# The first layer's accumulator of value products is copied out of PSUM by VectorE instead of ScalarE

## The chip, the cores and the metric

The kernel runs on one core of a Trainium2 chip. The time is that of the device in microseconds, from start to end of one execution. Its engines work side by side, each with its own queue in fixed order, and wait for one another by semaphores: TensorE (PE in the profile, its weight loads PEld), VectorE (DVE), ScalarE (ACT), GpSimd (POOL) and SyncE (SP), which issues DMAs. PSUM is the memory that TensorE writes its results to, here eight banks of 128 partitions x 512 numbers of 4 bytes.

## What is computed

Two transformer layers over x of 16 batches x 512 tokens x 128 features, each attention plus a feed-forward part beside it:

```python
xn = layernorm(x)
x = x + attn0(xn) + ffn0(xn)   # 16 heads of 8, low-rank q/k/v with RMS norm, causal
xn = layernorm(x)
x = x + attn1(xn) + ffn1(xn)   # 16 heads of 8, a bias by position; composed weights, gelu
# in attention, per head: softmax(q @ k.T * scale + mask or bias) @ v, heads joined, projected
```

## The kernel before

The batches run one after another, a batch's work being spread over several "bodies" of 64 slots. A body is four head groups u = 0 to 3, each with four blocks of keys kt = 0 to 3, each with four steps j; slot 16u + 4kt + j. Every engine walks through the same slots by its own code and issues what is due there, so the order on each engine is written out by hand. For 14 bodies only the first layer runs, three more carry both layers in alternating slots, and the rest is the second layer alone. A slot of the first layer has

- on TensorE: at j = 0 the value products of the group before (L639, into pv_acc, one PSUM bank, 128 x 512; eight matmuls per block of keys), then a tile of scores transposed (L655, into one of three banks) and a tile of scores for the maxima (L680 and L692, into one of four banks);
- on ScalarE: the exponential of a bank of scores (L961, into probs);
- on VectorE: the reduction of a bank to row maxima (L1193, L1198, L1199, L1202, into maxs);
- on GpSimd: the causal mask on the probabilities (L1315).

The rest hangs on named slots: layernorm (L862 on ScalarE at slot 12), the transposes of the accumulator's copy (L705 on TensorE, named OA at slot 17 and OB at slot 49), the division by the row sums that follows (L1067 and L1074 on VectorE), the square root of the RMS norm (L897 on ScalarE at slot 42, which needs a table load before and after), the scaling by it (L1123 on VectorE at slot 43), the sum with x and its stores by GpSimd (L1281, L1283, L1259).

The value products of two head groups (a pair) add up in pv_acc. When the fourth block of the second group is done, at slot 12 (for the pair that ended with the body before) and at slot 44, the bank is copied to accS in SBUF. Only then may TensorE start the next pair there, at slots 16 and 48 (it waits for acc_taken), and transpose accS. The copy waits for the last value product and for the older transposes that read accS. There are two copies per batch and layer: 32 in the first, 32 in the second. A reduction of VectorE at slot 12 or 44 itself doesn't exist; the nearest ones come at slots 11, 13 and 15.

Of the kernel before, what the change touches and what calls it, by code (L numbers as in the profile page):

```python
# [21 lines left out]
NT = T // P  # L22
G = 4
NG = H // G
# [4 lines left out]
VW, PAIR = 32, 2  # L29
# [73 lines left out]
def max_column(j, qt):  # L103
    return 2 * NT * (j % E) + NT * (j // E) + qt


def place(layer, kt, j):

    if layer == 1:
        return G * kt + j, 0, T  # L110
    width = T - P * kt
    row, column = {0: (j, 0), 1: (G + j, 0), 3: (G + j, T - P), 2: (2 * G + j % 2, 2 * P * (j // 2))}[kt]
    return row, column, width
# [181 lines left out]
def wait(eng, sem, value):  # L295

    if not isinstance(value, int) or value > 0:
        eng.wait_ge(sem, value)
# [12 lines left out]
def build(nc, a, out):  # L311
# [14 lines left out]
    with ExitStack() as ctx:  # L326
        def sb(name, shape, dt=F32):
            return ctx.enter_context(nc.sbuf_tensor(name, shape, dt))
# [7 lines left out]
        acc = ctx.enter_context(nc.psum_tensor("pv_acc", [P, T], F32))  # L336
# [17 lines left out]
        accS = sb("accS", [P, T])  # L354
# [477 lines left out]
        def _(act):  # L832
# [8 lines left out]
            def body(B):  # L841
                s, layer = S[B.layer], B.layer

                full, taken = s["work_full"], s["act_taken"]
# [94 lines left out]
                for u in range(NG):  # L939
                    for kt in range(NT):  # L940
                        for j in range(G):
                            eo, eu = (-1, NG - 1) if u == 0 else (0, u - 1)
                            if j == 0 and kt == NT - 1 and u % PAIR == 0 and B.has(eo):
                                act.wait_ge(s["pv_done"], B.count(NG * NT, NT * eu + NT, eo))
                                if layer == 1 and B.number == 0 and u == PAIR:
                                    act.wait_ge(S[0]["work_full"], Body(0, LAST).use("OA").full)
                                if B.has(-1):
                                    transposed = B.use("OA") if u else Body(layer, B.number - 1).use("OB")
                                    act.wait_ge(full, transposed.full)
                                fn(accS[:], acc[:], ACT.Copy).then_inc(s["acc_taken"], 1)  # L950
                            number, pack, tile = TILES[layer][4 * kt + j]
                            if B.has(0) and tile == pack[-1]:
                                if layer == 0 and number == 0:
                                    wait(act, s["pv_done"], B.count(NG * NT, NT * (u - 1)))
                                if layer == 1 and B.number == 0 and u == 0 and number in (0, PACK_ROWS):
                                    act.wait_ge(S[0]["pv_done"], NG * NT * NB - (NT if number == 0 else 0))
                                if layer == 1 and j == 0:
                                    wait(act, s["pv_done"], B.count(NG * NT, NT * (u - 1) + kt + 1))
                                act.wait_ge(s["st_ready"], B.count(NG * EXPS[layer], EXPS[layer] * u + number + 1))
                                row = place(layer, *tile)[0] + (PACK_ROWS * (u % 2) if layer == 0 else 0)  # L960
                                fn(probs[:, row, :], st[:, B.use(("st", u, number)).bank, :], ACT.Exp, scale=SCALE  # L961
                                   ).then_inc(s["exp_done"], 1)
                            other(16 * u + 4 * kt + j)
                            yield

            run(body(Body(0, FIRST)))
            act.wait_ge(setup_pool, 5)
            run(body(Body(0, FIRST + 1)))
            act.wait_ge(stage_free, 3)
            run_first_layer(act, body)  # L970
            run_both_layers(body)
            run_second_layer(act, body)
# [4 lines left out]
        def _(dve):  # L977
            v = nc.vector
# [65 lines left out]
            def body(B):  # L1044
                s, layer = S[B.layer], B.layer

                full, taken = s["work_full"], s["dve_taken"]
# [129 lines left out]
                for u in range(NG):  # L1177
                    for kt in range(NT):
                        so, su = (0, u + 2) if u < 2 else (1, u - 2)
                        for j in range(NT):  # L1180
                            m = NT * kt + j
                            number, pack, tile = TILES[layer][m]
                            if layer == 1 and B.number + so == 0 and su < 2 and m == 0:
                                dve.wait_ge(S[0]["msplit"], 2 * NG * NB - 2 + 2 * su)
                            if B.has(so) and m == 0:
                                wait(dve, s["msplit"], B.count(2 * NG, 2 * (su - 1), so))
                            if B.has(so) and layer == 0 and tile == pack[-1]:
                                dve.wait_ge(s["s1_ready"], B.packs(0, su, number + 1, so))
                                bank = s1[:, Body(0, B.number + so).use(("max", su, number)).bank, :]
                                jh, qt = BESIDE[0][m]  # L1190
                                column = max_column(jh, qt)
                                if qt == 1:
                                    v.reduce_max(maxs[:, su % 2, column - NT:column + 1:NT],  # L1193
                                                 bank.rearrange("p (b n) -> p b n", b=2), AX_X
                                                 ).then_inc(s["red_done"], 1)
                                elif qt == 0:
                                    wide = max_column(jh, 2)
                                    v.reduce_max(maxs[:, su % 2, wide:wide + 1], bank[:, 0:3 * P], AX_X)  # L1198
                                    v.reduce_max(maxs[:, su % 2, column:column + 1], bank[:, 3 * P:T], AX_X  # L1199
                                                 ).then_inc(s["red_done"], 1)  # L1200
                                else:
                                    v.reduce_max(maxs[:, su % 2, column:column + 1], bank, AX_X  # L1202
                                                 ).then_inc(s["red_done"], 1)
                            if B.has(so) and layer == 1:
                                reduce_tiles(Body(1, B.number + so), su, m)
                            other(16 * u + 4 * kt + j)
                            yield

            for slot, _ in enumerate(body(Body(0, FIRST))):
                if slot == OTHER_WORK[0]["NORM"][0]:  # L1210
                    set_up()
# [188 lines left out]
```

## Time and profile before

| | |
|---|---|
| median of 3 runs | 1710.07 us (1704.68 to 1724.67) |
| profiled execution, its own time | 1698.95 us |
| its span, first to last instruction | 1697.2 us |
| mean granted TensorE clock | 0.974 of full speed |
| first layer alone | from about 100 to 700 us of the span |

The profile is of one execution. A row of a timeline gives the start in us from the start of the span and the duration in us; where several instructions of a line stand together, the duration is that of the group. The rows of one engine overlap a little: an instruction's end and the start of the next are pipelined. The bracket says how long the engine was idle before the row and whose work ended the idle time.

### The profile page before, as it was taken

What the parts mean: (1) busy time and instruction counts of PE and PEld (TensorE: products, weight loads), DVE (VectorE), ACT (ScalarE), POOL (GpSimd) and SP (SyncE); (2) the same over time, 40 slices, a digit from 0 to 9 for tenths busy, and PEclk for the clock granted to TensorE, in tenths of its full rate; (3) what the DMA queues carried; (4) which work ended last, traced back from release to release, by engine and by line L of the source; (5) the groups of instructions that cost most, each with busy time, mean ns of one, the idle gap of its engine ahead of it and who ended that gap; (6) DMA issues with size and microseconds to landing.
All of it is one profiled execution on the core that took longest, in us unless ns stands there. A gap on an engine that the chain in (4) does not pass through costs nothing.

```text
span 1697.2 us, 33267 instructions
## 1 busy us (share of the span) xinstructions
PE 1499.7 (88%) x11850; PEld 624.7 (37%) x11850; DVE 1378.8 (81%) x2538; ACT 1290.5 (76%) x2550; POOL 935.7 (55%) x1176
## 2 busy tenths in 40 slices
PE   4778888888888888888899999999999999999995
PEld 2644444444444444433233323233333323332331
DVE  2378888888888888888888898888888888889880
ACT  2258878878878787766788788888888888888884
POOL 2135555555555555554655655566556656565565
PEclk9879999999999999999999999999999999999998
DMA  8332332232222223322321223123321233122300
GB/s 289 63 57 76 76 73 76 76 73 79 76 75 74 78 64 74 81 63 49 79 70 51 57 53 68 57 51 57 64 66 51 48 64 74 51 58 48 67 15 19
DMA packets 133125, 116.41 MB, mean 69 GB/s; under 512 B 16856, under 2 KB 125664, under 8 KB 132960
## 3 DMA queue, kind: packets, MB, share of 16 engines
q1 hardware_dynamic: 126272, 100.64, 25.3%
q0 software_dynamic: 4096, 8.40, 1.5%
q10 hardware_dynamic: 2592, 5.24, 0.9%
q8 instruction: 95, 1.56, 0.4%
q14 instruction: 70, 0.57, 0.1%
HBM read 79.63 MB, written 33.55 MB: 67 GB/s over the span
## 4 chain that ended last, share of the span: by engine, by line
PE 53%; ACT 16%; DVE 14%; POOL 8%; issue 5%; DMA 3%; SPq 1%; DVEq 0%; POOLq 0%; ACTq 0%
PE pv_acc L639 16%; PE scores_transposed L655 13%; ACT probs L961 7%; PE scores_transposed L793 4%; PE scores_transposed L765 4%; PE scores_for_max L676 4%; DVE maxs L1171 3%; POOL x_between_layers L1259 2%; PE scores_for_max L801 2%; PE scores_for_max L705 2%; DVE maxs L1174 2%; POOL probs L1315 1%; DVE maxs L1202 1%; ACT xn L862 1%; POOL parts L1242 1%
## 5 line engine op out<-in xcount | busy, mean ns | idle before, releaser
L961 ACT ACTIVATE probs<-scores_transposed 128x512 f32<-128x512 f32 x1664 | 909.0, 600 | 178.3 <-PE scores_transposed L655 170.5
L655 PE MATMUL scores_transposed<-stacks 62*128 62x512 bf16 (+3 forms) x2048 | 583.5, 346 | 50.5 <-ACT probs L961 34.8
L639 PE MATMUL pv_acc<-probs,vals 128*32 128x512 f32 (+3 forms) x4096 | 469.3, 530 | 49.3 <-POOL probs L1315 25.4
L1341 POOL TENSOR_TENSOR probs<-probs,near_bias 128x512 f32<-128x512 f32 x256 | 329.6, 1290 | 327.0 <-ACT probs L961 326.1
L1171 DVE TENSOR_REDUCE maxs<-scores_for_max 128x2 f32<-128x1024 f32 x325 | 390.7, 1221 | 77.0 <-PE scores_for_max L676 76.3
L655 PEld LDWEIGHTS scores_transposed<-stacks 62*128 62x128 bf16 x2048 | 155.5, 94 | 603.8 <-ACT probs L961 304.0
L676 PE MATMUL scores_for_max<-stacks 60*128 60x512 bf16 x1024 | 328.7, 384 | 11.4 <-DVE maxs L1171 9.1
L1174 DVE TENSOR_REDUCE maxs<-scores_for_max 128x1 f32<-128x512 f32 x374 | 245.9, 684 | 16.1 <-PE scores_for_max L676 12.0
L680 PE MATMUL scores_for_max<-stacks 60*128 60x512 bf16 (+3 forms) x1024 | 248.9, 312 | 10.9 <-DVE maxs L1199 6.1
L1202 DVE TENSOR_REDUCE maxs<-scores_for_max 128x1 f32<-128x512 f32 x256 | 175.4, 685 | 82.4 <-PE scores_for_max L692 80.0
L1315 POOL TENSOR_SCALAR_AFFINE_SELECT probs<-probs 128x512 f32<-128x512 f32 x256 | 159.6, 638 | 76.7 <-ACT probs L961 76.4
L692 PE MATMUL scores_for_max<-causal_halves,ident_halves 64*128 64x128 bf16 (+2 forms) x1280 | 187.1, 233 | 0.0
L1198 DVE TENSOR_REDUCE maxs<-scores_for_max 128x1 f32<-128x384 f32 x256 | 140.2, 548 | 34.1 <-PE scores_for_max L692 33.2
L639 PEld LDWEIGHTS pv_acc<-probs,vals 128*32 128x32 f32 x4096 | 82.4, 108 | 159.7 <-issue 104.6
L692 PEld LDWEIGHTS scores_for_max<-causal_halves,ident_halves 64*128 64x128 bf16 x1280 | 112.9, 98 | 36.0 <-issue 5.1
L1242 POOL TENSOR_TENSOR parts<-rest,parts 128x512 bf16<-128x512 f32 x64 | 75.6, 1182 | 65.3 <-ACT parts L937 64.9
L676 PEld LDWEIGHTS scores_for_max<-stacks 60*128 60x128 bf16 x1024 | 77.6, 93 | 34.8 <-DVE maxs L1171 21.3
L1193 DVE TENSOR_REDUCE maxs<-scores_for_max 128x2 f32<-128x512 f32 x128 | 87.5, 684 | 0.9 <-PE scores_for_max L692 0.8
L680 PEld LDWEIGHTS scores_for_max<-stacks 60*128 60x128 bf16 x1024 | 77.6, 95 | 16.7 <-DVE maxs L1199 9.4
L1270 POOL TENSOR_TENSOR rstd<-mv,minus_half 128x4 f32<-128x4 f32 x32 | 33.4, 1042 | 82.5 <-DVE mv L1090 82.5
L1259 POOL DMA_INDIRECT out_dram<-x_new,slots_now x64 | 64.7, 1010 | 21.0 <-issue 10.6
L1259 POOL DMA_INDIRECT x_between_layers<-x_new,slots_now x64 | 65.1, 1017 | 17.0 <-issue 12.6
(131 smaller groups left out, 1982.8 us busy)
## 6 DMA issues: line engine op xcount, KB each, us to landing
stacks<-parts_scratch SPq DMA_DIRECT2D x768, 64.0 KB
parts_scratch<-parts SPq DMA_DIRECT2D x64, 384.0 KB, 2.6
x_tile<-in_L_attn_x_dram SPq DMA_DIRECT2D x16, 256.0 KB, 2.8
probs<-in_fc_B_dram ACTq DMA_DIRECT2D x1, 4096.0 KB, 19.5
stage_a<-in_fc_A_T_dram SPq DMA_DIRECT2D x1, 4096.0 KB, 16.8
stacks<-mT SPq DMA_DIRECT2D x256, 4.0 KB
x_res<-in_L_attn_x_dram SPq DMA_DIRECT2D x16, 256.0 KB, 3.3
x_tile<-x_between_layers SPq DMA_DIRECT2D x16, 256.0 KB
```

Of the source, the lines that this page charges most:

```text
L639: last = mm(acc[VW * j:VW * j + VW, q0:T], columns[:, first:first + VW], probs[:, row, column:column + width], start=(kt == 0 and pu % PAI ...
L655: last = mm(st[:, bank, column:column + T - q0], ks[p][rows, h, P * kt:P * kt + P], qs[p][rows, h, q0:T], start=True, stop=True)
L676: mm(bank, qs[p][rows, h, P * qt:P * qt + P], ks[p][rows, h, :], start=True, stop=True).then_inc(s["s1_ready"], 1)
L680: mm(bank[:, column:column + P * (qt + 1)], qs[p][rows, h, P * qt:P * qt + P], ks[p][rows, h, 0:P * (qt + 1)], start=True, stop=False, ski ...
L692: last = mm(masked, ident_halves[half, n, :], mask, start=False, stop=(n == 1), skip_group_check=True)
L961: fn(probs[:, row, :], st[:, B.use(("st", u, number)).bank, :], ACT.Exp, scale=SCALE).then_inc(s["exp_done"], 1)
L1171: v.reduce_max(maxs[:, su % 2, :].rearrange("p (e x) -> p e x", e=E)[:, :, column], s1[:, bank - 1:bank + 1, :], AX_X).then_inc(s["red_don ...
L1174: v.reduce_max(maxs[:, su % 2, column:column + 1], s1[:, bank, :], AX_X).then_inc(s["red_done"], 1)
L1202: v.reduce_max(maxs[:, su % 2, column:column + 1], bank, AX_X).then_inc(s["red_done"], 1)
L1259: g.indirect_dma_start(x_dst[layer], bass.IndirectOffsetOnAxis(slots_now[:, layer, t:t + 1], 0), x_new[:, t, :], None).then_inc(s["x_store ...
L1315: g.affine_select(out=diag, in_=diag, compare_op=ALU.is_ge, fill=0.0, base=0, pattern=[[0, G], [1, P]], channel_multiplier=-1).then_inc(s[ ...
L1341: g.tensor_tensor(diag, diag, near_bias[:, kt, :].unsqueeze(1).broadcast_to([P, G, P]), ALU.mult).then_inc(s["emul_pool"], 1)
```

## The change

The 32 copies of the first layer go from ScalarE's loop to VectorE's, at the same slots (kt = 3, j = 0, even u), ahead of what either engine does in that slot, with the same waits. The second layer's stay on ScalarE.

```diff
--- before.py
+++ after.py
@@ -940,7 +940,7 @@
                     for kt in range(NT):
                         for j in range(G):
                             eo, eu = (-1, NG - 1) if u == 0 else (0, u - 1)
-                            if j == 0 and kt == NT - 1 and u % PAIR == 0 and B.has(eo):
+                            if layer == 1 and j == 0 and kt == NT - 1 and u % PAIR == 0 and B.has(eo):
                                 act.wait_ge(s["pv_done"], B.count(NG * NT, NT * eu + NT, eo))
                                 if layer == 1 and B.number == 0 and u == PAIR:
                                     act.wait_ge(S[0]["work_full"], Body(0, LAST).use("OA").full)
@@ -1178,6 +1178,13 @@
                     for kt in range(NT):
                         so, su = (0, u + 2) if u < 2 else (1, u - 2)
                         for j in range(NT):
+                            eo, eu = (-1, NG - 1) if u == 0 else (0, u - 1)
+                            if layer == 0 and j == 0 and kt == NT - 1 and u % PAIR == 0 and B.has(eo):
+                                dve.wait_ge(s["pv_done"], B.count(NG * NT, NT * eu + NT, eo))
+                                if B.has(-1):
+                                    transposed = B.use("OA") if u else Body(layer, B.number - 1).use("OB")
+                                    dve.wait_ge(full, transposed.full)
+                                v.tensor_copy(accS[:], acc[:]).then_inc(s["acc_taken"], 1)
                             m = NT * kt + j
                             number, pack, tile = TILES[layer][m]
                             if layer == 1 and B.number + so == 0 and su < 2 and m == 0:
```

VectorE around slot 44 of a first-layer body, before (maxs are the reductions, the L1123 row the scaling by the root, L1067 the reciprocal of the row sums):

```order
L1110 SCALAR_TENSOR_TENSOR ffn<-fc,scores_for_max 128x512
L1123 TENSOR_TENSOR big<-big,rrms 128x4x256
L1198 TENSOR_REDUCE maxs<-scores_for_max 128x1
L1199 TENSOR_REDUCE maxs<-scores_for_max 128x1
L1198 TENSOR_REDUCE maxs<-scores_for_max 128x1
L1199 TENSOR_REDUCE maxs<-scores_for_max 128x1
L1202 TENSOR_REDUCE maxs<-scores_for_max 128x1
L1067 RECIPROCAL rsum<-scores_for_max 128x32
```

The same place after (the reductions' lines are 7 higher):

```order
L1110 SCALAR_TENSOR_TENSOR ffn<-fc,scores_for_max 128x512
L1123 TENSOR_TENSOR big<-big,rrms 128x4x256
L1187 COPY accS<-pv_acc 128x512
L1205 TENSOR_REDUCE maxs<-scores_for_max 128x1
L1206 TENSOR_REDUCE maxs<-scores_for_max 128x1
L1205 TENSOR_REDUCE maxs<-scores_for_max 128x1
L1206 TENSOR_REDUCE maxs<-scores_for_max 128x1
L1209 TENSOR_REDUCE maxs<-scores_for_max 128x1
```

The copy now stands between the scaling and four reductions.

ScalarE around slot 12, before (xn is the layernorm's result, vals the values for the next batch):

```order
L878 ACTIVATE fd<-scores_transposed 128x512
L961 ACTIVATE probs<-scores_transposed 128x512 x2
L950 ACTIVATE accS<-pv_acc 128x512
L862 ACTIVATE xn<-x_tile,minus_mean_rstd,rstd 128x128 x4
L961 ACTIVATE probs<-scores_transposed 128x512 x2
```

The same place after:

```order
L878 ACTIVATE fd<-scores_transposed 128x512
L961 ACTIVATE probs<-scores_transposed 128x512 x2
L862 ACTIVATE xn<-x_tile,minus_mean_rstd,rstd 128x128 x4
L961 ACTIVATE probs<-scores_transposed 128x512 x2
L889 ACTIVATE vals<-big 128x64x8
```

The copy is gone from between the exponentials and the layernorm. TensorE's order is the same in both kernels.

## Rows read from the trace of the kernel before

**Rows 1.** The page, busy time per engine (us, share of span, instructions).

```profile
PE 1499.7 (88%) x11850; PEld 624.7 (37%) x11850; DVE 1378.8 (81%) x2538; ACT 1290.5 (76%) x2550; POOL 935.7 (55%) x1176
```

**Rows 2.** View by tile, accS: duration in ns min/median/max; who waited (us, times).

```profile
L950 ACT ACTIVATE accS<-pv_acc x64: 591/598/628, 134.5 to 1678.7; 128x512 f32<-128x512 f32 x64
...
  PE pv_acc L639: 23.0, 14
```

**Rows 3.** View by line, L1030: the same read by VectorE, in the setup.

```profile
L1030 DVE COPY w<-pv_acc x1: 685/685/685, 50.7 to 50.7; 128x512 f32<-128x512 f32 x1
```

**Rows 4.** Chain that ended last, slots 43 to 48, body 4 (start us, us, what).

```profile
306.34 0.50 ACT accS L950
306.84 0.14 issue
306.98 1.06 PE pv_acc L639 x8
```

**Rows 5.** VectorE's timeline, same stretch (start, us, engine, line, instruction, [idle before <-releaser]).

```profile
305.20 1.22 DVE L1123 TENSOR_TENSOR big<-big,rrms 128x1024 f32<-128x1024 f32 x1
306.33 0.55 DVE L1198 TENSOR_REDUCE maxs<-scores_for_max 128x1 f32<-128x384 f32 x1
...
308.56 0.69 DVE L1202 TENSOR_REDUCE maxs<-scores_for_max 128x1 f32<-128x512 f32 x1 [0.81 <-PE scores_for_max L692]
```

**Rows 6.** TensorE's timeline, same stretch.

```profile
306.98 1.06 PE L639 MATMUL pv_acc<-probs,vals 128*32 128x512 f32 x8 [1.87 <-ACT accS L950]
```

**Rows 7.** VectorE's timeline, the same slots of body 3.

```profile
264.28 0.55 DVE L1198 TENSOR_REDUCE maxs<-scores_for_max 128x1 f32<-128x384 f32 x1
```

**Rows 8.** TensorE's timeline, the same slots of body 3.

```profile
260.23 0.28 PE L680 MATMUL scores_for_max<-stacks 60*128 60x256 bf16 x1 [0.66 <-DVE maxs L1199]
...
264.38 1.06 PE L639 MATMUL pv_acc<-probs,vals 128*32 128x512 f32 x8 [1.33 <-ACT accS L950]
```

**Rows 9.** Chain that ended last, slots 11 to 17 of body 5.

```profile
327.07 0.49 ACT accS L950
327.56 1.51 ACT xn L862 x4
329.08 0.50 ACT probs L961
...
329.62 0.28 PE scores_transposed L655
```

**Rows 10.** VectorE's timeline, same stretch.

```profile
327.14 0.56 DVE L1198 TENSOR_REDUCE maxs<-scores_for_max 128x1 f32<-128x384 f32 x1
...
329.44 0.69 DVE L1202 TENSOR_REDUCE maxs<-scores_for_max 128x1 f32<-128x512 f32 x1 [0.88 <-PE scores_for_max L692]
330.53 0.36 DVE L1067 RECIPROCAL rsum<-scores_for_max 128x32 f32<-128x32 f32 x1 [0.39 <-PE scores_for_max L705]
```

**Rows 11.** TensorE's timeline, same stretch.

```profile
327.86 1.07 PE L639 MATMUL pv_acc<-probs,vals 128*32 128x512 f32 x8 [0.54 <-POOL probs L1315]
328.86 0.39 PE L655 MATMUL scores_transposed<-stacks 62*128 62x512 bf16 x1
...
329.62 0.28 PE L655 MATMUL scores_transposed<-stacks 62*128 62x256 bf16 x1 [0.28 <-ACT probs L961]
...
329.84 0.66 PE L705 MATMUL scores_for_max<-ident,accS 128*128 128x128 f32 x4
```

**Rows 12.** Busy us (instructions) of PE, PEld, DVE, ACT, POOL; PEclk; DMA share; GB/s.

```profile
348.60:354.60 6.00, 5.03 (x34) 2.21 (x35) 3.79 (x10) 3.33 (x7) 4.08 (x6) 0.72 0.01 3
```

**Rows 13.** TensorE's timeline, the wait at slot 48 of bodies 5 and 6.

```profile
349.57 1.64 PE L639 MATMUL pv_acc<-probs,vals 128*32 128x512 f32 x8 [1.86 <-ACT accS L950]
...
393.70 1.07 PE L639 MATMUL pv_acc<-probs,vals 128*32 128x512 f32 x8 [1.26 <-ACT accS L950]
```

**Rows 14.** VectorE's timeline where both layers run, around slot 12 of body 15.

```profile
765.67 0.55 DVE L1198 TENSOR_REDUCE maxs<-scores_for_max 128x1 f32<-128x384 f32 x1
```

**Rows 15.** TensorE's timeline, same stretch.

```profile
765.51 1.07 PE L639 MATMUL pv_acc<-probs,vals 128*32 128x512 f32 x8 [0.47 <-issue]
```

## The prediction, written before the changed kernel ran

> **What bounds the kernel now.** I read the busy time per engine first [rows 1]: TensorE 88%, VectorE 81%, ScalarE 76% of the span. No engine is full, so the place of the moved work decides, not its amount. The view by tile comes next [rows 2]: one copy on ScalarE takes 598 ns (median), and TensorE has waited for it 14 times, 23.0 us in all. VectorE has done the same instruction once, in the setup, in 685 ns [rows 3]. Then the chain that ended last. Followed stretch by stretch through the first layer, it has 23 of the 32 first-layer copies on it, each with about 0.50 us of its own [rows 4, 9]; the rest of a copy's 0.6 us overlaps its neighbours. Read alone this says: take 23 x 0.5 = 11.5 us off the chain. The timelines of VectorE and TensorE around the copies tell how much of it really comes back. There are two kinds of copy in each batch. I call the one at slot 12 early and the one at slot 44 late.
>
> **The late copy (slot 44).** ScalarE makes it right after the two table loads around the square root, and TensorE stands still until it is done: 1.87 us before the value products of slot 48 [rows 6]. These start 0.14 us after the copy's end [rows 4]. Now where would VectorE put it? Behind the scaling by the root (L1123) and ahead of the reductions of slot 45. VectorE had no idle time in front of that place: L1123 starts at 305.20 and the next reduction at 306.33 [rows 5]. So the copy would start at 306.33, end 0.685 later at 307.02, and with the same 0.14 the products start at 307.16 instead of 306.98: 0.18 us later. ScalarE's freed 0.5 us buys nothing here, since it waits for TensorE's next scores anyway. In eight of the fourteen late copies before the two layers overlap the distance is this one (the reduction comes 0.09 to 0.13 after the old copy's start; losses 0.18 to 0.22, together 1.6 us). In five, bodies 1, 3, 6, 12 and 13, VectorE is 0.56 us later than that relative to ScalarE, TensorE too (its wait is 1.26 to 1.33 instead of 1.85). Body 3: the reduction starts at 264.28, so the copy ends at 264.97 and the products start at 265.11 instead of 264.38 [rows 7, 8]: 0.73 lost. VectorE is the later one there, TensorE had waited for one of its reductions before [rows 8]. The five lie between 0.73 and 0.79, together 3.8 us. Body 0 lies between them with 0.36. Late copies together: **+5.7 us**. The five were not on the chain, so up to 0.3 of each loss may be slack: 4.2 is the lower bound. What follows doesn't hide it: the chain goes on from these products through the transposes and the parts of Q and K to the next batch. VectorE has room for the longer queue: it idles 0.81 us before the reduction at 308.56 [rows 5].
>
> **The early copy (slot 12).** ScalarE makes it between an exponential and the four layernorm instructions of L862, all on the chain [rows 9], and TensorE waits 0.28 us for the exponential behind them [rows 11]. VectorE would start the copy at 327.14, where it now starts a reduction [rows 10], and end at 327.83; 0.14 on, the value products of slot 16 start at 327.97 instead of 327.86, where they now wait for GpSimd's mask [rows 11]. That is 0.11 lost on TensorE. But the exponential ends 0.49 earlier, so the scores of slot 17 come at 328.86 + 0.11 + 0.23 (two such score matmuls in a row start 0.23 apart) = 329.20 instead of 329.62: 0.42 gained. The transposes of accS start as much earlier, 329.42 for 329.84, and end at 330.08. VectorE meanwhile has its reductions 0.60 later, its wait of 0.88 at 329.44 shrinks, and the reduction there (329.55, 0.60 to the next start) frees it at 330.15. Its reciprocal of the row sums starts then, instead of 330.53 [rows 10]: 0.38 gained. The chain goes on from there through GpSimd's sum and stores, which were waiting for VectorE. The pattern is the same to 0.01 us in all 13 early copies of bodies 1 to 13. Early copies: 13 x 0.38 = **-4.9 us**.
>
> **Where both layers run (five copies, bodies 14 to 16).** At body 15 the products of slot 16 start at 765.51 with no wait for the copy. VectorE reaches its place only at 765.67 [rows 14, 15], so they would start at 765.67 + 0.69 + 0.14 = 766.50, a loss of 0.99. The other four lose 0.1 to 0.3 or nothing by the same rule, and ScalarE's freed time is on the chain once more, at body 16 (about -0.3). I take **+1.1 us**. The bounds: -2.5 (five times 0.5 freed) to +3.
>
> **The waits that move with the copy.** VectorE now waits for the value products of slot 44 or 12 and for an older transpose. Both are long past: TensorE is already idle [rows 6], or past its slot 15 [rows 11]. Behind the waiting instruction on VectorE stand the reductions of slots 13 and 15, whose banks TensorE needs again only from slot 49 (17) on. ScalarE loses these waits and gains nothing, as they weren't binding. TensorE, GpSimd, the DMA queues and layer 1 keep their instructions.
>
> **Sum.** +5.7 - 4.9 + 1.1 = **+1.9 us**, on the profiled execution's 1698.95: 1700.9. The three runs shown are 1704.68, 1710.07 and 1724.67, all above the profiled one, so I carry the difference to their median: 1710.07 + 1.9 = **1712 us**. About 1% (17 us) is what a measurement of this kernel can tell from no change, and this is far inside.
>
> The page "VectorE: DVE Perf Modes" of the Trainium skill, in its section on the TRN2 errata, gives 120 + N cycles at 0.96 GHz for VectorE's read of PSUM and 172 + N at 1.2 GHz for ScalarE's, and says that ScalarE sits closer to PSUM. For 512 columns that is an estimate of 658 and 570 ns, so it speaks against this move by 88 ns a copy; this case's rows have 685 and 598, 87 apart. By the page's 658 the sum would be 1 us smaller; the rows decide.
>
> **Rivals.**
> (a) ScalarE's relief carries in full and VectorE's later copy is made good, because its queue before slot 44 moves up too: 11.5 us gained at most, and with the late copies merely free the early 4.9: 1698.5 to 1705. For it: the chain's own shares. Against it: VectorE had no idle time before 305.20, and that queue begins behind TensorE's work, which moves with everything else.
> (b) The early gain doesn't carry, since another chain of the same length (GpSimd's masks, the stores) is close behind: the early copies then cost 0.11 each, 1.4 us, and the sum is 5.7 + 1.4 + 1.1 = 8.2: 1718. For it: the wait of TensorE there is only 0.28. Against it: GpSimd waits for VectorE's result in that place.
> (c) TensorE's clock, the case that is slower. At the late copy it idles 1.3 to 1.87 us, and with the change 2.05 in all fourteen (1.87 + 0.18, 1.33 + 0.73). After three of the fourteen waits, all three among those of 1.82 to 1.87 us, the clock was at 1.2 GHz for some us: mean 0.72 of full speed in 6 us [rows 12], the eight-matmul group 1.64 instead of 1.06 [rows 6, 13]. It cost about 1.5 us: body 5 to 6 took 393.70 - 349.57 = 44.13 us [rows 13], body 3 to 4 306.98 - 264.38 = 42.60 [rows 6, 8]. If it fell at all fourteen, 11 more x 1.5 = 17 us come on top: 1729, slower by 1.1%. It decides from the point where the idle time or the thin stretch ahead of it is a little longer. Against it: five more waits of the same 1.85 us left the clock alone. The Trainium skill's page "TensorE: Matmul & The Clock Gate", Part 1, has the clock gated by how busy the engine has been of late, and idle gaps drop it to the lower level; the trace agrees as far as its three falls go, and the rule points to this rival.
> (d) The copies don't move. The order of the instructions excludes it: 32 copies less on ScalarE, 32 more on VectorE.
>
> **How the numbers follow.** Forecast, the sum within 4 us: 0.50. (a) 0.18, (b) 0.15, (c) 0.12 (half of it with only some falls, 1715 to 1722), none of them 0.05. The range runs from 1698, which takes in (a) nearly whole and the lower bound of the mixed stretch, to 1724, which takes in (b) and a third to a half of the extra falls of the clock. Faster by over 1% would need 17 us, more than all copies give: 0.04, for what I don't see. Slower by over 1%: 0.10, from (c) and from (b) with VectorE's delay passed on everywhere. Within 1%: 0.86.
>
> **What the profile after would show.** Right: copies of 0.68 us on VectorE; TensorE's wait before the late products at 2.05 us in nearly all batches, ended by VectorE's copy; no wait of TensorE for the exponential at slot 17; 42.4 us from batch to batch where the late copy cost 0.18, and 43.0 where it cost 0.75; ScalarE 19 us less busy, VectorE 22 us more. Wrong: TensorE's wait before the late products under 1.8 us (VectorE's queue moved up, a), reciprocals no earlier against the exponentials (b), a granted clock well below 0.974 (c). What could upset all of it: that which makes VectorE 0.56 us later in five batches may come in none or in all fourteen, which is worth -2.9 to +5 us.

## The result, and the profile after

| | before | after |
|---|---|---|
| median | 1710.11 us of 16 runs (1698.32 to 1728.06) | 1722.25 us of 16 runs (1715.44 to 1736.35) |
| ratio, 95% interval | 1 | 1.009 [1.0066, 1.0113] |
| profiled execution, its span | 1698.95, 1697.2 us | 1721.62, 1719.8 us |
| granted TensorE clock | 0.974 | 0.965 |

A ratio, here and below, is that of the executions within 1.5% of the fastest of their kernel, so it isn't always that of the medians beside it. The change costs 12 us, 0.9%. The forecast had 1712.0 within 1698 to 1724, and no difference that a measurement can tell. The page after, busy time per engine, answers to [rows 1]:

```profile
PE 1510.0 (88%) x11850; PEld 628.7 (37%) x11850; DVE 1400.5 (81%) x2570; ACT 1275.4 (74%) x2518; POOL 932.0 (54%) x1176
```

VectorE has 21.7 us more, ScalarE 15.1 less, and TensorE, whose instructions are the same, is 10.3 us busier. That is the first sign of where the time went: the same matmuls took longer. The view by tile, accS, answers to [rows 2]:

```profile
L1187 DVE COPY accS<-pv_acc x32: 679/680/683, 129.6 to 840.0; 128x512 f32<-128x512 f32 x32
...
  PE pv_acc L639: 28.6, 14
```

TensorE waits for the copy in the same 14 places, 28.6 us instead of 23.0. At the late copy of body 3, the chain after, which answers to [rows 4]:

```profile
261.02 0.61 DVE accS L1187
261.63 0.14 issue
261.77 1.06 PE pv_acc L639 x8
```

VectorE and TensorE there, answering to [rows 5, 6]:

```profile
259.81 1.22 DVE L1123 TENSOR_TENSOR big<-big,rrms 128x1024 f32<-128x1024 f32 x1
260.94 0.68 DVE L1187 COPY accS<-pv_acc 128x512 f32<-128x512 f32 x1
261.54 0.54 DVE L1205 TENSOR_REDUCE maxs<-scores_for_max 128x1 f32<-128x384 f32 x1
```

```profile
261.77 1.06 PE L639 MATMUL pv_acc<-probs,vals 128*32 128x512 f32 x8 [2.05 <-DVE accS L1187]
```

The copy begins behind the scaling without idle time, 0.83 later come the products, and TensorE has waited 2.05 us, all as forecast. It is 2.05 or 2.06 in 13 of the 14 batches. The early copy, VectorE and TensorE at slots 12 to 17 of the next body, answering to [rows 10, 11]:

```profile
281.89 0.68 DVE L1187 COPY accS<-pv_acc 128x512 f32<-128x512 f32 x1
...
284.89 0.36 DVE L1067 RECIPROCAL rsum<-scores_for_max 128x32 f32<-128x32 f32 x1
```

```profile
282.68 1.06 PE L639 MATMUL pv_acc<-probs,vals 128*32 128x512 f32 x8 [0.57 <-POOL probs L1322]
...
283.91 0.28 PE L655 MATMUL scores_transposed<-stacks 62*128 62x256 bf16 x1
...
284.19 0.66 PE L705 MATMUL scores_for_max<-ident,accS 128*128 128x128 f32 x4
```

TensorE's wait for the exponential at slot 17 is gone (the row at 283.91 has no bracket), and the reciprocal starts 0.70 after the transposes' start, where it was 0.69 [rows 10, 11].

Then the stretches behind the late copies, 10 us each from 1.8 us ahead of the products (busy us and instructions of PE, PEld, DVE, ACT, POOL; PEclk; DMA share; GB/s), as in [rows 12], bodies 3 to 5:

```profile
259.97:269.97 10.00, 8.20 (x90) 4.22 (x91) 9.01 (x20) 7.80 (x16) 5.82 (x8) 1.00 0.08 27
302.24:312.24 10.00, 8.20 (x67) 3.74 (x68) 7.66 (x16) 6.49 (x13) 5.43 (x8) 0.83 0.01 2
346.03:356.03 10.00, 8.20 (x50) 3.68 (x51) 6.79 (x14) 5.82 (x12) 5.38 (x8) 0.66 0.01 2
```

The clock stayed up once, and then it was at its lower level (1.2 GHz) for part of the stretch: TensorE is busy for the same 8.20 us, but with 67 and 50 instructions instead of 90. I call it a fall where such a stretch shows less than 1.00. There are 9 falls behind the 14 late copies, and 4 before the change (the prediction had found three; a fourth shows in the same view at 566.75). From products to products a batch takes 42.27 us without a fall (261.77 to 304.04), 43.79 with one (304.04 to 347.83), 44.97 with the long one. A fall costs 1.5 us, a long one 2.7.

**Where the 22.6 us between the two spans lie.** The first late products start at 130.40 instead of 135.19, -4.8; profiles of either kind of kernel have 129 to 132 or 135 to 140, so this isn't the change. The next 13 batches take 583.97 us instead of 562.22, +21.8: the undisturbed batch 13 x (42.27 - 42.60) = -4.3; falls 7 x 1.5 + 2 x 2.7 = 16 against 7, +9; four long waits of TensorE for the stacks that a DMA brings, 17.1 us (6.82, 1.87, 2.35, 6.07), against 1.7 and 1.0, +14; the rest is what the batches around them lose. From the 14th late products to the end 1005.4 instead of 999.8, +5.6. The longest of the waits for stacks, in TensorE's timeline:

```profile
433.10 0.61 PE L655 MATMUL scores_transposed<-stacks 62*128 62x512 bf16 x1 [6.82 <-DMA stacks<-mT]
```

So two suspects stood beside each other: the clock, and the loads. The profiled executions are 22.7 us apart and the medians 12.1: single executions differ by such waits. How the 12.1 divide between the two isn't measured; the experiments show what each does by itself.

### The profile page after: what moved, and what is told of

Read it like the earlier page. It is cut to its first block, busy times and chain, and to the rows that moved or that the text cites. A ratio compares the mean times of both kernels' runs of the same rounds, so it can differ in the third digit from the quotient of the medians.

```text
span 1719.8 us, 33267 instructions
## 1 busy us (share of the span) xinstructions
PE 1510.0 (88%) x11850; PEld 628.7 (37%) x11850; DVE 1400.5 (81%) x2570; ACT 1275.4 (74%) x2518; POOL 932.0 (54%) x1176
## 4 chain that ended last, share of the span: by engine, by line
PE 56%; DVE 20%; ACT 12%; POOL 4%; issue 4%; DMA 3%; SPq 1%; DVEq 0%; POOLq 0%; ACTq 0%
PE pv_acc L639 16%; PE scores_transposed L655 13%; ACT probs L961 6%; PE scores_transposed L793 4%; PE scores_transposed L765 4%; PE scores_for_max L676 4%; DVE maxs L1171 3%; DVE maxs L1209 3%; DMA stacks<-mT 2%; PE scores_for_max L705 2%; PE scores_for_max L801 2%; DVE maxs L1174 2%; DVE rest L1147 1%; ACT parts L937 1%; PE scores_for_max L692 1%
## 5 line engine op out<-in xcount | busy, mean ns | idle before, releaser
L639 PE MATMUL pv_acc<-probs,vals 128*32 128x512 f32 (+3 forms) x4096 | 472.5, 533 | 55.0 <-DVE accS L1187 28.6
L676 PE MATMUL scores_for_max<-stacks 60*128 60x512 bf16 x1024 | 328.9, 385 | 14.7 <-DVE maxs L1171 12.1
L692 PE MATMUL scores_for_max<-causal_halves,ident_halves 64*128 64x128 bf16 (+2 forms) x1280 | 188.9, 235 | 0.0
L692 PEld LDWEIGHTS scores_for_max<-causal_halves,ident_halves 64*128 64x128 bf16 x1280 | 113.9, 99 | 37.5 <-issue 7.5
L793 PE MATMUL scores_transposed<-w,big 128*128 128x128 f32 x512 | 74.1, 288 | 0.0
```

The lines of the kernel that those rows point to most:

```text
L639: last = mm(acc[VW * j:VW * j + VW, q0:T], columns[:, first:first + VW], probs[:, row, column:column + width], start=(kt == 0 and pu % PAI ...
L676: mm(bank, qs[p][rows, h, P * qt:P * qt + P], ks[p][rows, h, :], start=True, stop=True).then_inc(s["s1_ready"], 1)
L692: last = mm(masked, ident_halves[half, n, :], mask, start=False, stop=(n == 1), skip_group_check=True)
L793: last = mm(work[:, 0:D], big[:, f, P * t:P * t + P], w2[:, f, :], start=(f == 0), stop=(f == NF - 1))
```

## The experiments

Theory F (for fall): the late copy costs little by itself, but it lengthens TensorE's wait before the late products, from 1.2 to 1.9 us up to 2.05, and at this length the clock falls in most batches. Its rivals are that the copies' own places on the path cost the time (P), that the slow loads come with the move (D; R has them slow whatever the kernel), and, last, that something else about the move to VectorE makes the clock fall (M). "Waits" below are TensorE's before the 14 late products.

**1 and 2. One copy of the two.** VectorE's condition `u % PAIR == 0` becomes `u == 0` (early alone) or `u == 2` (late alone), and ScalarE keeps the other:

```diff
-  if layer == 0 and j == 0 and kt == NT - 1 and u % PAIR == 0 and B.has(eo):
+  if layer == 0 and j == 0 and kt == NT - 1 and u == 0 and B.has(eo):
```

Early alone:

> Only the early copies (slot 12) go to VectorE, the late ones (slot 44) stay on ScalarE. Theory F (the loss is TensorE's clock, which falls in the thin stretch around the late copy when TensorE's wait there grows from 1.3-1.87 to 2.05 us): the wait stays at 1.85 us, the clock falls after about as few late copies as before (4 of 14), and the early gain of about 0.35 us a batch shows: 4 to 6 us less than before, ratio about 0.997. Theory D (the moved copies as such make the rows of maxima, mT, reach the stacks later, and TensorE waits for that DMA): waits for that DMA of several us here too, ratio 1.000 to 1.005. Theory P (only the path counts, as predicted): 4.9 us less, ratio 0.997.

Measured: 1732.69 us, before in the same job 1726.53 (17 runs from 1692.89 to 1739.98), ratio 1.017 [1.006, 1.029].

Late alone:

> Only the late copies go to VectorE, the early ones stay on ScalarE. Theory F: TensorE waits 2.05 us in most batches, 8 or more falls of the clock among 14, ratio 1.010 to 1.014, a little above the full change since the early gain is missing. Theory D: ratio about 1.004. Theory P: 5.7 us more, ratio 1.003, with periods of 42.8 and no more falls than before.

Measured: 1744.49 us, ratio 1.023 [1.009, 1.036]. The job's runs of the kernel before spread over 47 us, and the profile of the first has six waits for stacks, 34 us in all, with an undisturbed batch of 42.2. By the medians of all executions the ratios are 1.004 and 1.010. The falls are as F has them, 4 and 10 of 14, and so is the order (late alone is the worse), but early alone came out slower, where F and P had it faster. The long waits are what theory D has. The spread leaves the sizes open, and these two alone settle nothing.

**3 and 4. TensorE kept busy through the wait.** The last tile of scores ahead of the wait is computed ten times more into the same bank, at slot 47:

```diff
+  if layer == 0 and u == 2 and 4 * kt + j == NT * G - 1 and B.has(0):
+      scores_again(u, 10)      # the same matmul, start=True, same bank
```

In the changed kernel:

> The changed kernel, with ten repetitions of one score matmul (same result, 0.16 us each) on TensorE in the last slot before the late copy is waited for, so that 1.6 us of the 2.05 us of idle time are work. Theory F: hardly a fall of the clock after late copies, periods of 42.3 us, ratio to before 0.99 to 1.00 (8 to 9 falls of 1.5 us gone: about 12 us less than the changed kernel). Theories D and P: the clock is not what cost the time, ratio stays at 1.006 to 1.010.

In the kernel before:

> The kernel before, with the same ten repetitions. Theory F: its 4 or so falls go too, 5 to 6 us less, ratio 0.996 to 0.998. Against it: no change, or slower, if the repetitions delay the exponentials or the reductions behind them.

Measured: 1729.85, ratio 1.017 [1.011, 1.022], and 1714.49, ratio 1.004 [0.997, 1.011]. Not one fall in either profile (28 waits, of at most 0.64 us), but the changed kernel's has six waits for stacks, 33 us. The absence of falls is as F says. The ratios are above what F gave (the medians of all executions give 1.002 and 0.993), so the time doesn't yet speak for it: it is drowned by the loads. These had to go.

**5 and 6. Both kernels once more, unchanged.**

> The kernel before, unchanged, for a second profile of it. Theory F (clock): falls after 3 to 5 of its 14 late copies. Theory D (the moved copies make TensorE wait for the stacks and their rows of maxima at slot 32): no wait of over 5 us for a DMA. Theory R (the rate of those loads is low in some batches whatever the kernel; a rate of some 70 GB/s in the 8 us after their start gives a wait of 5 to 9 us, 90 gives 0 to 2.5, over 100 none): such waits can be here too.

> The changed kernel, unchanged, once more. Theory F: falls after 8 to 10 of 14 late copies, ratio of medians 1.005 to 1.010. Theory D: two or more waits of over 5 us for the stacks. Theory R: their number is that of the slow loads, none to five, with no relation to the kernel.

Measured: 1702.89 (one execution) and 1747.19 us (4 runs), before 1720.86; the second's ratio 1.021 [1.011, 1.031]. The profile of the kernel before has waits of 1.18 to 1.30 in twelve batches with no fall, one of 1.79 with none, and one of 2.27, behind a slow load, with a fall. It is the same kernel in all, and only its longest wait has one (the granted clock was back at 1.00 before this wait):

```profile
484.15 1.48 PE L639 MATMUL pv_acc<-probs,vals 128*32 128x512 f32 x8 [2.27 <-ACT accS L950]
```

The changed kernel has 13 falls in 14. F had given 3 to 5 and 8 to 10 and a ratio of 1.005 to 1.010, so it missed both counts and the size: the waits of the kernel before differ from one execution to another (mostly 1.85 in the first profile, 1.2 here), and so, then, does what the change costs.

**7 and 8. Light loads.** The first layer's stack loads bring one head of eight, so seven eighths of these loads are left out of the work:

```diff
-  sp.dma_start(dst[row:row + HD, :, :], heads[e])
+  some = slice(0, 1 if layer == 0 else H // E)
+  sp.dma_start(dst[row:row + HD, some, :], heads[e][:, some, :])
```

Before, light:

> The kernel before, but each load of the first layer's stacks brings one head of eight (the other heads keep old contents, so scores are those of other data): no wait for the stacks can be left. Theories R and D: the waits for that DMA are gone, the runs lie closer together, 1675 to 1700 us. Theory F: still falls after some late copies.

Changed, light:

> The changed kernel with the same light loads. Compared with the kernel before with light loads, Theory F: slower by the extra falls alone less the better path, 5 falls x 1.5 - 4 = 3 to 8 us, waits of 2.05 us before 13 or 14 late products. Theory D (the change costs by the DMA alone): 4 us faster, since the stacks no longer come late. Theory P: 1 to 2 us slower without more falls.

Measured: 1688.77 (ratio 0.985 [0.976, 0.995]) and 1714.92 (0.999 [0.996, 1.003]). There are no long waits for stacks left in the first layer, and the difference hasn't shrunk: 26.2 us. The loads aren't needed for it. F had given only 3 to 8 us. The two profiled spans are 22.5 us apart, and 21.0 of it lie in the 13 batches: about 16 are falls and 5 the undisturbed batch (43.0 instead of 42.62). TensorE's products in a batch of each:

```profile
346.19 1.07 PE L641 MATMUL pv_acc<-probs,vals 128*32 128x512 f32 x8 [1.23 <-ACT accS L952]
```

```profile
395.62 1.93 PE L641 MATMUL pv_acc<-probs,vals 128*32 128x512 f32 x8 [2.06 <-DVE accS L1189]
```

The eight matmuls take 1.93 us instead of 1.07. One fall in 14 in the light kernel before, 11 in the light changed one.

**9. Early alone, light.**

> Only the early copies on VectorE, with the light loads of the first layer's stacks (one head of eight is loaded, so the scores are of other data); to be compared with the kernel before with light loads, 1688.8 us. Theory F (clock): TensorE's wait before the late products stays at 1.2 to 1.9 us, 0 to 4 falls of the clock, and the early gain of 0.35 us in 13 batches shows: 1682 to 1686 us. A rival E (the early copy is what costs, through the reductions behind it): 1695 us or more.

Measured: 1695.59, ratio 0.992 [0.988, 0.996]. The undisturbed batch takes 42.14 us, so the early copy itself isn't what costs, but part of the gain was eaten: the waits were 1.91 to 1.93 in twelve batches, and there were 5 falls, more than F gave. The median is the one that rival E gave, and the profiled execution, 1690.43, lies between the two forecasts. In twelve of these batches TensorE doesn't wait for VectorE some 4 us before, as it mostly does in experiment 7 (0.7 to 0.8 us), so it comes to its wait for the late copy earlier and the wait is longer. That VectorE's earlier start in this execution (the last section) is the reason wasn't tested.

**10. Both copies, light, with the fill of experiment 3.**

> The changed kernel with light loads and ten repeated score matmuls on TensorE in front of its wait for the late copy. With light loads alone the changed kernel took 1714.9, the kernel before 1688.8. Theory F: no falls of the clock at late copies, periods of 42.9 to 43.0 us, 1692 to 1700 us: some 18 of the 26 us come back, and the 4 to 11 that stay are the later start of the late products. Against F: the clock doesn't fall but the time stays above 1708.

Measured: 1687.21 (1685.91 to 1690.85), ratio 0.987 [0.982, 0.992]. TensorE's timeline, and the stretch around the products:

```profile
338.13 1.78 PE L669 MATMUL scores_transposed<-stacks 62*128 62x384 bf16 x10
340.34 1.07 PE L641 MATMUL pv_acc<-probs,vals 128*32 128x512 f32 x8 [0.43 <-DVE accS L1202]
```

```profile
338.54:348.54 10.00, 9.57 (x99) 4.78 (x98) 9.01 (x20) 7.79 (x16) 5.82 (x8) 1.00 0.08 26
```

The wait is 0.43, there are no falls, and every batch takes 42.27 or 42.28 us. The median is 28 us under that of the light changed kernel and at that of the light kernel before, but these are of another job; against its own job's kernel before each, 0.987 is 0.012 under 0.999, about 20 us. It is also below the 1692 to 1700 that F gave. In the profiles the 13 batches are 27.5 us shorter than in experiment 8: 18 are its falls, and 9.5 are the batch of 42.27 instead of 43.0, a difference between executions that the last section shows and that isn't the fill's (experiment 3, with the fill, has 42.98). So with the clock held the moved copies cost nothing against the 42.62 of the kernel before in an execution of the one kind, and 0.4 us a batch, 5 us in all, in one of the other.

**11 and 12. The late copy earlier on ScalarE.** It stands right behind the square root, ahead of the second table load, instead of behind an exponential at slot 44:

```diff
   other(16 * u + 4 * kt + j)
+  if layer == 0 and 16 * u + 4 * kt + j == OTHER_WORK[0]["ROOT"][0] and B.has(0):
+      ...                               # the same waits
+      fn(accS[:], acc[:], ACT.Copy).then_inc(s["acc_taken"], 1)
```

Early copy on ScalarE:

> The kernel before with the late copy still on ScalarE, but ahead of the second table load and of one exponential (right behind the square root of slot 42). Theory F with the path: TensorE's wait before the late products shrinks from 1.2-1.9 to 0.1-0.4 us, the late products start 1.1 to 1.8 us earlier, the exponential behind them 0.5 later, no falls after late copies: 0.5 to 1.2 us a batch, 8 to 20 us less than before, ratio 0.988 to 0.995. Against it: another chain of equal length takes over (GpSimd's mask before slot 52) and the ratio stays at 0.998 to 1.000.

Early copy on VectorE:

> The same late copy on ScalarE ahead of the table load, and the early copies on VectorE. Theory F with the path: the early gain of 0.35 us a batch on top, ratio 0.985 to 0.993. Against it: like the kernel with the late copy ahead alone, or slower by VectorE's longer queue.

Measured, with full loads: 1689.18, ratio 0.989 [0.985, 0.993], and 1689.69, ratio 0.987 [0.984, 0.990]. ScalarE and TensorE of the first:

```profile
303.89 1.28 ACT L897 ACT_TABLE_LOAD   x1
305.19 0.31 ACT L897 ACTIVATE rrms<-ssq 128x128 f32<-128x128 f32 x1
305.48 0.60 ACT L968 ACTIVATE accS<-pv_acc 128x512 f32<-128x512 f32 x1
306.10 1.28 ACT L961 ACT_TABLE_LOAD   x1
```

```profile
306.22 1.07 PE L639 MATMUL pv_acc<-probs,vals 128*32 128x512 f32 x8
...
308.13 0.37 PE L655 MATMUL scores_transposed<-stacks 62*128 62x512 bf16 x1 [0.84 <-ACT probs L961]
```

The products don't wait for the copy any more; one idle stretch of 2 us became two short ones with the products between them. No falls in either, 41.92 us a batch, and 41.50 with the early copy on VectorE. Both ratios lie where F gave them. Nothing is left out in either: with the full work they are the fastest of all these versions, 1.1 and 1.3% under the kernel before.

**13 to 16. The wait lengthened without a move.** So far the wait had been shortened or filled in the changed kernel. Here the copies stay on ScalarE, and the late one is made in pieces; loads are light:

```diff
+  pieces = 4 if layer == 0 and u == PAIR else 1        # 8 in the second
+  for piece in range(pieces):
+      cols = slice(T // pieces * piece, T // pieces * (piece + 1))
+      last = fn(accS[:, cols], acc[:, cols], ACT.Copy)
+  last.then_inc(s["acc_taken"], 1)
```

> The kernel before with the late copy left on ScalarE but made in four pieces of 128 columns instead of one of 512, and with one head of eight in the first layer's stack loads (the other heads' loads are left out). Nothing moves to VectorE. Four pieces should take 0.3 to 0.9 us longer than one copy (the four layernorm instructions of 128 columns took 1.51 us together, 0.38 each, against 0.60 for one of 512), so TensorE's wait before the late products becomes 1.6 to 2.1 us in the batches in which it was 1.2 to 1.3. Theory F, that the length of this wait alone decides how often TensorE's clock falls: falls after 3 to 10 of the 14 late copies, each 1.5 us, against 1 of 14 with one piece. Rival M, that it is the move to VectorE and what this does to the other engines: falls after 0 to 2, as with one piece. The longer copy itself costs 14 x 0.3 to 0.9 = 4 to 13 us over 1689 by both; F adds 5 to 15.

> The same with the late copy in eight pieces of 64 columns on ScalarE; everything else is the kernel before with the light stack loads. The copy should take 1 to 2.3 us longer than in one piece, TensorE's wait becomes 2.2 to 3.6 us, longer than the 2.05 of the changed kernel. Theory F: the clock falls after 11 to 14 of the 14 late copies, each 1.5 us or more, and the granted clock of the whole is near 0.967; the period from batch to batch grows by the longer copy and by 1.5 on top. Rival M: 0 to 2 falls, clock near 0.979, the period grows by the longer copy alone.

> The kernel with the late copy in eight pieces, and ten repeated score matmuls on TensorE at slot 47, which fill 1.6 us of its wait. The copy is as late as without them, so this prices the delay of the products alone. Theory F: no falls of the clock, the period shorter by 1.5 us or more than without the fill, 15 to 25 us in the whole. Rival M: the same time with and without the fill, within 3 us.

> Only the early copies on VectorE, with the light stack loads and the ten repeated score matmuls at slot 47, so that the clock is held. It prices the early copies without falls. Theory F: no falls, a period of 42.14 as in the undisturbed batches of the same kernel without the fill, against 42.62 of the kernel before, so 14 x 0.45 = 6 us less than the kernel before with light loads (1688.8): 1682, and 7 us less than the same kernel with its five falls. Rival G, that the early gain is given back elsewhere (in the batches where both layers run, or in the second layer): 1687 to 1689.

| | median us | ratio, interval | waits, us | falls | undisturbed batch |
|---|---|---|---|---|---|
| four pieces | 1700.44 | 0.993 [0.990, 0.997] | 1.46 to 1.58 (3), 2.01 to 2.06 (11) | 0 of 3, 9 of 11 | 42.78 |
| eight pieces | 1711.47 | 1.001 [0.997, 1.005] | 1.73, 1.83, then 2.24 to 2.33 (12) | 1 of 2, 10 of 12 | 43.03 |
| eight pieces, fill | 1691.03 | 0.991 [0.988, 0.994] | 0 to 0.68 | 0 of 14 | 43.01 |
| early on VectorE, fill | 1685.33 | 0.988 [0.983, 0.994] | 0 to 0.23 | 0 of 14 | 42.15 |

The longer copy costs 0.2 and 0.4 us a batch by itself, 2 to 6 us in all; with eight pieces the time is 22.7 us above the light kernel before (of another job), and the fill takes 20.4 back at the same lateness. Three batches of the kernel with four pieces, from TensorE's timeline:

```profile
392.31 1.07 PE L641 MATMUL pv_acc<-probs,vals 128*32 128x512 f32 x8 [1.51 <-ACT accS L955]
...
435.10 1.06 PE L641 MATMUL pv_acc<-probs,vals 128*32 128x512 f32 x8 [2.04 <-ACT accS L955]
...
477.88 1.52 PE L641 MATMUL pv_acc<-probs,vals 128*32 128x512 f32 x8 [2.05 <-ACT accS L955]
```

and the stretches around the last two, in the view by windows:

```profile
433.30:443.30 10.00, 8.20 (x90) 4.22 (x91) 8.43 (x19) 8.41 (x20) 5.83 (x8) 1.00 0.09 28
476.08:486.08 10.00, 8.20 (x67) 3.74 (x68) 7.07 (x15) 7.12 (x17) 5.46 (x8) 0.83 0.00 1
```

No copy is on VectorE, and the clock falls as in the changed kernel. F stands; the falls don't need the move itself, so rival M is out as their cause. A wait of 2.04 us left the clock alone and the next, of 2.05, didn't (of the three waits of 2.04 in this profile two had a fall), so there is chance in it and no sharp limit. (The Trainium skill's "TensorE: Matmul & The Clock Gate", Part 1, has the activity watched in a window that runs freely and isn't reset by the kernel; by that rule two like gaps may end differently, and these rows agree.) The last kernel came out 3 us above the 1682 that F gave it: its undisturbed batches take the expected 0.47 us less each than those of the light kernel before, and what follows the 14th late products takes 1006.2 us instead of 1001.5. That is rival G's place and half its size.

**The falls, counted over ten profiles without the fill** (before, after, 1, 5, 6, 7, 8, 9, 13, 14; 140 late waits; that of experiment 2, whose execution was 14 us above its median, isn't counted; it has 10 falls in 14):

| wait of TensorE, us | times | with a fall |
|---|---|---|
| 0.74 to 1.58 | 41 | 0 |
| 1.69 to 1.93 | 30 | 11 |
| 2.01 to 2.33 | 69 | 57 |

With the fill or the earlier copy the waits are 0 to 0.68 us, 98 of them, without a fall.

The rows of the first line tell one thing more. In all 41 of them TensorE had already stood idle for VectorE for 0.60 to 1.25 us some 4 us earlier, and the two idle times add up to 1.98 to 2.18 us, more than the waits of the second line with their 11 falls. So in these rows the falls go with the unbroken wait, not with the idle time in sum; no experiment broke a wait in two and changed nothing else.

## Why the prediction was wrong

**The step that failed** is the one on rival (c), TensorE's clock: "Against it: five more waits of the same 1.85 us left the clock alone." I took it for a reason that 0.2 us more would be left alone as well. It was miscounted: of the eight waits of 1.82 to 1.87 four had a fall and four hadn't, not three and five. And it showed only that 1.85 lies in the range in which a fall is a matter of chance, 11 times in 30 here. At 2.05 the chance is 57 in 69. The mechanism, its place, its price of 1.5 us and its sign were in the prediction; I gave it 0.12 and forecast the sum without it. Rival (c) has 1729 with a fall at all fourteen; by its own price 9 to 13 falls give 1721 to 1727, and 1722.25 was measured. That the two agree is in part luck: the falls differ from one execution to another in both kernels, and so do the waits for stacks. A better reading of the same rows was at hand: none in five at 1.3 us, half at 1.85, so more than half at 2.05, in all fourteen places at once.

**Wait, place and copy.** Right: 0.68 us, products 0.83 after the copy's start, the wait at 2.05, ended by VectorE's copy.

**Early copies.** Forecast -0.38 a batch. Measured 42.60 - 42.15 = 0.45 with the late copy left alone, so it carries, and rival (b) is out. Rival (a) is out too, since VectorE's queue before slot 44 didn't move up against TensorE's.

**Late copies.** This term was off too. Forecast 0.18 or 0.75 a batch, with periods of 42.4 and 43.0. Both kinds came, but not as a mix by batch: all 13 batches of one execution are of one kind (the last section). In the profile after it is 42.27 - 42.15 = 0.12; in experiments 6 and 8 42.98 to 43.01, that is 0.85. This is the caveat at the prediction's end, worth -2.9 to +5 there; the 13 batches of the two kinds are -4.3 and +5 us against before. The kernel before was profiled only in executions of the second kind, so the -4.3 compares unlike ones and the +5 like ones.

**Both layers.** Forecast +1.1 (-2.5 to +3). What follows the 14th late products takes 999.8, 1002.4 and 1001.5 us in three profiles of kernels with nothing moved and 1005.4, 1006.1 and 1004.3 in three with both copies moved: about +4, above my upper bound. A 14th fall is in it in some, but experiment 10, without falls, has 1006.7 as well. So have the kernels with pieces, 1003.7 to 1006.9, and early alone has 1001.0 in experiment 9 and 1006.2 in 16. So what of it the moved copies cost stays open.

**Sum.** The +1.9 left the clock out. For what it counts, experiment 10 lies 1.6 us below the light kernel before, which looks fair, but its terms were off both ways: over 13 batches the early copies gave 5.9 us (forecast 4.9), the late ones cost 1.6 or 11 by the kind of execution (forecast 5.7), the rest about 4 (forecast 1.1). That they cancel in the first kind is luck; in the second the sum is about +9. ScalarE's busy time fell by 15.1 us, not 19, which touches nothing.

**Open.** Why some of the stack loads are slow. Waits of 5 to 9 us for them come in profiles of both kernels: counted from 100 us on, 2 in the four with full loads and no copy moved to VectorE (before, 4, 5, 11), but 17 in the six with one moved or both (after, 1, 2, 3, 6, 12). That looks as if the change made them likelier, but single executions of either kernel differ much, and no experiment tests it. The light kernels show only that a difference as large comes without them.

## What to carry to other kernels

All of it comes from one kernel. Where TensorE already stands idle for nearly 2 us after light work and some of these waits cost it its clock, a few tenths more are not worth a few tenths: price such a change as (more falls) x (what one costs), and read the chance from the waits of different lengths that the trace already has. The reverse is cheap to try: take the last instruction before the wait out from behind other work (here one copy ahead of a table load, 1.1% gained), or give TensorE harmless work there. To tell a clock effect from a path effect, fill the wait and leave everything else as it is.

## What I had not expected of the hardware

A reduction of VectorE just ahead of slot 32 waits for two matmuls of TensorE (L692). TensorE's rows are alike in all profiles, but VectorE starts 0.36 to 0.37 us after their start in every batch of five profiles (after, 9, 10, 11, 12), and 1.0 to 1.15 after it in all others, but for their first batch and one odd row. The same changed kernel has both. In the profile after, TensorE's and VectorE's timelines:

```profile
291.25 0.33 PE L692 MATMUL scores_for_max<-causal_halves,ident_halves 64*128 64x256 bf16 x2
```

```profile
291.62 0.56 DVE L1205 TENSOR_REDUCE maxs<-scores_for_max 128x1 f32<-128x384 f32 x1 [1.06 <-PE scores_for_max L692]
```

and in experiment 6, the same kernel:

```profile
295.39 0.33 PE L692 MATMUL scores_for_max<-causal_halves,ident_halves 64*128 64x256 bf16 x2
```

```profile
296.48 0.56 DVE L1205 TENSOR_REDUCE maxs<-scores_for_max 128x1 f32<-128x384 f32 x1 [1.79 <-PE scores_for_max L692]
```

An execution of the changed kernel has 42.27 us a batch with the first and 43.0 with the second (experiments 3, 6, 8), 9 us in all. With the early copies alone it makes no difference (42.14 and 42.15). What decides it I don't know; that it is fixed for an execution is read from one profile of each kernel and two of the changed one. It goes with the job as much as with the kernel: all four profiles of experiments 9 to 12, one job on one chip, are of the first kind, and all twelve of experiments 1 to 8 and 13 to 16, on two other chips, of the second. So it may belong to the chip.

The other one: the clock's answer to a gap is steep, from no fall in 41 waits up to 1.58 us to 57 in 69 from 2.01 on, and a gap of about the same sum that is broken in two, as in those 41, had none.
